# First scores of a cross-attention computed in the draining steps of the stage before it

## The reference, cut to what matters

```python
x = x + _L0_attn_ref(_layernorm(x), ...)               # linear attention: (q k^T / scale) v, no softmax
x = x + _L0_xattn_ref(ctx, ctx, _layernorm(x), ...)    # ctx has 77 rows for each sequence
...
v, k, q = (_feature_map(x, fm_w, fm_b) for x in (v, k, q))   # z = x @ fm_w.T + fm_b; concat(exp(z), exp(-z))
scores = einsum('nqhd,nkhd->nhqk', q, k) / sqrt(128.)        # 16 heads, 16 features each after the map
attn = softmax(scores, axis=-1)
out = einsum('nhql,nlhd->nqhd', attn, v).reshape(...) @ fc_w.T + fc_b
```

## Time and profile before

| | us |
|---|---|
| median of three runs | 450.48 |
| range of the runs | 449.48 to 454.25 |
| the profiled execution, its own time | 453.67 |
| its span in the profile | 451.9 |
| busy: PE, DVE, ACT, POOL | 381.6, 279.4, 255.0, 195.8 |

### The profile page before, as it was taken

One profiled execution on the slowest core, in us unless ns is written; L12 is line 12 of the kernel. 1 busy time (PEld: TensorE's weight loads), 2 busy tenths in 40 slices (PEclk: granted clock), 3 DMA queues, 4 the chain that ended last, 5 costly groups with the idle time before them and its releaser, 6 DMA issues.

```text
span 451.9 us, 10394 instructions
## 1 busy us (share of the span) xinstructions
PE 381.6 (84%) x3684; PEld 290.9 (64%) x3685; DVE 279.4 (62%) x837; ACT 255.0 (56%) x611; POOL 195.8 (43%) x280
## 2 busy tenths in 40 slices
PE   2789787897458998999989998899999978888894
PEld 1476565564226787888888887675566657667662
DVE  4667988878537688787777754727733334444436
ACT  4778889876530776777757777355632223333311
POOL 1497577753005445544630000000577717676620
PEclk9999999998755999999989999989999999999999
DMA  8962335458517667566610000000051137777529
GB/s 273 349 186 56 125 102 159 137 179 248 159 70 195 172 168 190 151 175 173 181 57 4 8 4 4 0 1 1 31 188 55 54 97 230 241 240 236 181 80 316
DMA packets 45050, 61.83 MB, mean 137 GB/s; under 512 B 7308, under 2 KB 40972, under 8 KB 43388
## 3 DMA queue, kind: packets, MB, share of 16 engines
q1 hardware_dynamic: 33400, 37.63, 27.1%
q0 software_dynamic: 4832, 20.37, 15.9%
q10 hardware_dynamic: 6768, 3.18, 2.9%
HBM read 43.34 MB, written 20.59 MB: 141 GB/s over the span
## 4 chain that ended last, share of the span: by engine, by line
PE 59%; DVE 19%; ACT 10%; issue 6%; DMA 5%; ACTq 1%; POOL 0%; DVEq 0%; SPq 0%; POOLq 0%
PE bank L743 7%; PE bank L732 6%; PE bank L1301 4%; PE bank L1356 3%; PE bank L1310 3%; PE bank L1311 3%; PE bank L705 3%; DVE res_q L348 3%; ACT xn L406 3%; DVE mx L819 3%; PE bank L767 2%; PE bank L584 2%; DMA t_row<-sorted_in 2%; PE bank L611 2%; ACT t_hT L1238 2%
## 5 line engine op out<-in xcount | busy, mean ns | idle before, releaser
L910 ACT ACTIVATE prob<-bank 77x512 f32<-77x512 f32 x128 | 74.4, 595 | 23.7 <-PE bank L732 23.5
L1282 POOL DMA_INDIRECT sorted_in<-h_rows,pos_s x32 | 31.5, 985 | 82.3 <-ACT h_rows L1215 73.7
L819 DVE TENSOR_REDUCE mx<-bank 128x5 f32<-128x385 f32 (+1 forms) x96 | 54.9, 576 | 18.6 <-PE bank L705 15.8
L1287 POOL DMA_INDIRECT routed<-t_y,t_no x47 | 45.4, 966 | 27.9 <-DVE t_y L1155 18.8
L732 PE MATMUL bank<-qst,kst 99*77 99x128 bf16 x512 | 50.8, 222 | 0.7 <-DMA qst<-mT 0.4
L1211 ACT ACTIVATE s_g<-bank 128x512 f32<-128x512 f32 x32 | 19.1, 598 | 47.3 <-PE bank L1311 33.7
L732 PEld LDWEIGHTS bank<-qst,kst 99*77 99x77 bf16 x512 | 39.0, 117 | 8.2 <-ACT prob L910 4.0
L667 POOL DMA_DIRECT2D qst<-qparts x36 | 18.2, 505 | 53.8 <-DMA kst<-kparts 34.2
L705 PE MATMUL bank<-kst,qst 96*128 96x77 bf16 x512 | 36.2, 208 | 5.8 <-DVE mx L819 3.1
L1065 DVE TENSOR_TENSOR act<-bank,s_g 128x512 f32<-128x512 f32 x24 | 16.5, 688 | 36.8 <-ACT s_g L1211 36.8
L1238 ACT COPY t_hT<-bank 128x128 f32<-128x128 f32 x47 | 12.5, 265 | 39.5 <-PE bank L1347 35.5
(11 more groups left out here) (162 smaller groups left out, 932.3 us busy)
## 6 DMA issues: line engine op xcount, KB each, us to landing
qst<-qparts POOLq DMA_DIRECT2D x36, 256.0 KB, 3.5
t_w<-in_expert_w SPq DMA_DIRECT2D x47, 192.0 KB, 2.8
qparts<-qpart SPq DMA_DIRECT2D x16, 384.0 KB, 3.9
kst<-kparts POOLq DMA_DIRECT2D x36, 154.0 KB, 4.1
kparts<-kpart SPq DMA_DIRECT2D x16, 231.0 KB, 3.7
sorted_in<-in_fill SPq DMA_DIRECT2D x1, 3102.0 KB, 12.9
t_row<-sorted_in ACTq DMA_DIRECT2D x47, 66.0 KB, 2.1
qst<-qparts SPq DMA_DIRECT2D x12, 256.0 KB, 4.4
```

Source lines behind the costliest of these rows:

```text
L819: v.tensor_reduce(mx[:, b % JA, h0:h1], bank[n % 2][:, 0:(h1 - h0) * KEYS].rearrange("p (h k) -> p h k", k=KEYS), AX.X, ALU.max, negate=Tr ...
L910: a.activation(prob[n % PROBS][:].rearrange("p c t -> p (c t)"), bank[2 + n % 2][0:KEYS], ACT.Exp, scale=SCORE_SCALE).then_inc(s["expd"], 1)
L1282: p.indirect_dma_start(out=sorted_in, out_offset=bass.IndirectOffsetOnAxis(ap=pos[:, b:b + 1].bitcast(U32), axis=0), in_=h_rows[:, b], in_ ...
L1287: p.indirect_dma_start(out=routed, out_offset=bass.IndirectOffsetOnAxis(ap=t_no[r][:].bitcast(U32), axis=0), in_=t_y[r][:], in_offset=None ...
```

## The change

Five things are edited.

- **The first scores move.** The scores of b = 0 to 3 (64 matmuls in 12 units), their maxima, the first two `parts`, the first `turn_shift` and the first `copy_shift` go from the head of stage 3 into steps 6, 7 and 8. The functions themselves stay the same, except that the first shift is transposed into bank 2.
- **The order of the sends.** SP sends the shift rows of pairs 0 and 1 before the query parts of group 7. These parts get a buffer of their own (`qhome`, on the memory of the key parts).
- **The waits for DRAM.** ACT and SP no longer wait for the last query parts at the head of stage 3. POOL loads the six query parts of group 2 without it, then waits for all, then loads the six key parts in one go, and goes on with group 3.
- **The matmuls without use** (before five, L781, ahead of the first `shifted`) are now 3 and 1 in step 7 and 4 in step 8 (`keep_streaming`, 256 columns each).
- **DVE's copy of half of V** (L379) stands ahead of `mask_products` and `query_residuals`, in the steps that have both a `front` and a `back` (steps 0 to 5).

```diff
             def step(first, front, middle, back, last):      # DVE
...
                     statistics(g, 1, "stat2", "mean2")
+                    if g >= NG - 2:
+                        for u in range(3):
+                            maxima(v, 2 * (g - (NG - 2)), u)
...
+                if front is not None and back is not None:
+                    g = front
+                    v.wait_ge(s["vp"], g + 1)
+                    v.tensor_copy(values_of(g, 1), turned_keys(g, 1)).then_inc(s["v_ready2"], 1)
                 if middle is not None:
                     mask_products(middle)
                 if last is not None:
                     query_residuals(last)
-                if front is not None and back is not None:
-                    g = front
-                    v.wait_ge(s["vp"], g + 1)
-                    v.tensor_copy(values_of(g, 1), turned_keys(g, 1)).then_inc(s["v_ready2"], 1)
...
+                    if NG - 3 <= g < NG - 1:                  # g is last
+                        k = g - (NG - 3)
+                        for u in range(3):
+                            maxima(v, 2 * k + 1, u)
+                        if k == 0:
+                            v.wait_ge(s["ones_rows"], 1)
+                        parts(v, k)
...
             def query_high(g, hf):                            # ACT
-                if g >= 2:
+                if g == NG - 1:
+                    for par in range(2):
+                        a.wait_ge(k_sent[par][hf], NG // 2 * 16)
+                        a.wait_ge(k_sent[par][1 - hf], NG // 2 * 16)
+                elif g >= 2:
                     a.wait_ge(q_sent[g % 2][hf], g // 2 * 16)
...
                     normalise(back, 1, "bias2", xn2[back % 2], "xn2")
+                if back == NG - 1:
+                    copy_shift(a, 0)
...
+                    if g == NG - 3:                           # PE, g is last
+                        pe.wait_ge(s["v_ready"], NG)
+                        for u in range(3):
+                            scores(pe, 0, u)
+                    if g == NG - 2:
+                        scores(pe, 1, 2)
+                        for u in range(3):
+                            scores(pe, 2, u)
+                        turn_shift(pe, 0)
+                        for u in range(2):
+                            scores(pe, 3, u)
+                        keep_streaming(3)
+                    if g == NG - 1:
+                        scores(pe, 3, 2)
+                        keep_streaming(4)
...
                     i.then_inc(s["mwp"], 1)                   # g is middle
+                    if g == NG - 1:
+                        scores(pe, 1, 0)
+                        scores(pe, 1, 1)
...
                     i.then_inc(s["xT2p"], 1)                  # g is back
+                    if g == NG - 1:
+                        keep_streaming(1)
...
                     for hf in range(2):                       # SP, q is last
+                        if q == NG - 1 and hf == 0:
+                            send_shift(sp, 0)
+                            send_shift(sp, 1)
                         sp.wait_ge(s["qlo"], q * 2 + (hf + 1))
...
-            all_sent(p, NG // 2)                              # POOL
             p.wait_ge(s["vp"], NG)
-            for group in range(2, NG):
+            p.wait_ge(s["xT2"], NG)
+            for i in range(len(Q_PART)):
+                load_one(p, 2, i, qst, qparts, Q_PART)
+                if i < JP:
+                    add_bias(JA + i)
+            all_sent(p)
+            for i in range(len(K_PART)):
+                load_one(p, 2, i, kst, kparts, K_PART)
+            for group in range(3, NG):
```

More of the change, by code:

```diff
@@ L536, in pe_phase1, with keep_streaming @@
         def pe_phase1(pe):
+            def keep_streaming(n):
+                for _ in range(n):
+                    pe.matmul(bank[5][:, 0:2 * P], ident[:], second_pack[:, 0:2 * P], start=True, stop=True)
             def turn_x(g):
@@ L661, in shifts, with load_one @@
             return (g // 2 + 1) * (16 * JA)
+        def load_one(eng, group, i, dst, src, part):
+            eng.dma_start(dst[group % NBUF][i:ROWS:len(part)], src[group, part[i]]).then_inc(parts_in[i % 2], 16)
         def load(eng, group, i):
@@ new lines, in decoder_layer, with scores @@
+        SHIFT_BANK = (2, 7)
+        def scores(pe, b, u):
+            r, c = home(b // JA, b % JA)
+            h0, h1 = UNITS[u]
+            n = b * len(UNITS) + u
+            if u == 0 and b % JP == 0 and b < 2 * JP:
+                pe.wait_ge(early_in[b // JP], LOADS)
+            if u == 0 and b % JP == 0 and b >= 2 * JP:
+                for k in range(2):
+                    pe.wait_ge(parts_in[k], loads(b // JA))
+            if n >= 2:
+                pe.wait_ge(s["amax"], n - 1)
+            for h in range(h0, h1):
+                i = pe.matmul(bank[n % 2][:, (h - h0) * KEYS:(h - h0 + 1) * KEYS],
+                              qst[r][0:ROWS, h, c * S:(c + 1) * S], kst[r][0:ROWS, h, c * KEYS:(c + 1) * KEYS],
+                              start=True, stop=True)
+            i.then_inc(s["ap"], 1)
```

177 lines of the change are left out of this document (77 added, 100 removed), and 6 rows, old and new, of the table s.

## The result

The changed kernel took 445.63 us, the median of four runs (442.30 to 447.90), beside 452.37 us for the kernel before on the same chip (449.48 to 455.21). The ratio is 0.9862 with an interval of 0.9819 to 0.9906. A second sitting gave 445.33 us, 0.9764 [0.9692, 0.9837]. The kernel is faster by 1.4 to 2.4%, some 7 us. Forecast were 11.85 us, a time of 438.6; the 445.63 lies above the range of 435.8 to 444.0.

The account below looks back on a forecast made before the run. A serial tail, one engine at a time and mostly at 1.2 GHz, bounds the kernel until the first `shifted`. 2.2 + 10.55 - 0.9 = 11.85 us off the profiled 453.67, shifted to the median: 438.6 us, range 435.8 to 444.0.

Parts of the forecast that it names:

- T0: Start of the first `shifted`, head of stage 3: 146.95 us before, forecast 136.4 without the gain from V's copy.
- The copy of V, 2.2 us: Steps 1 to 5: copying in DVE's idle time brings the bias 0.60 us sooner; 4 x 0.40 + 0.60 = 2.2 us.
- 0 (another engine binds within 0.1 us): Lower bound on the gain from moving DVE's copy of V; the upper bound was 3.0 us.
- The tail, 10.55 us: Steps 6 to 8: scores moved into the serial tail bring T0 from 146.95 to 136.4, 10.55 us earlier.
- Step 7: DVE's order there delays the bias of group 7 from 123.45 to 129.0: the tail loses 5.5 us.
- The first rival (442.1): Step 8: the clock does not come back, T0 = 140.7, gain 8.4 us, time 442.1; chance 0.18.
- Given back, 0.9 us: After T0: DVE's first maximum of b = 4 comes late for PE; 0.9 us charged, between 0 and 1.5.
- DVE's debt: DVE enters stage 3 later relative to T0; its first b = 4 maximum at T0 + 2.9, PE wanting T0 + 2.1.
- Loads, nothing: POOL's query and key loads in stage 3 cost nothing; sequence 4's key loads have a thin cover of 1.0 us.
- Key loads late: Stage 3: sequence 4 waits 2.5 us for key loads, group 3 again as much; time 443.6, chance 0.10.
- POOL's loads pace: Stage 3: every group waits for its loads, 12.5 us over groups 3 to 7; time 454, chance 0.04.
- their rival: Head of stage 3: shift rows' signal comes behind POOL's query loads, T0 = 139.2, time 441.0; chance 0.10.

Follow-up runs that it names:

- the rearranged kernels: Changed kernel with DVE's addition, statistics and bias of group 7 ahead of the last b = 1 maximum: 444.84 us; DVE's later parts and maxima also reordered: 440.28 us.
- the filled changed kernel: Changed kernel plus three matmuls without use in TensorE's idle 1.20 us at the end of stage 3: 445.29 us, ratio to before 0.9805.
- The kernel with the maxima first: Changed kernel with DVE's first two maxima of b = 4 ahead of group 7's middle and low parts: 441.02 us, ratio to before 0.9722.
- the freed key loads: The kernel with the maxima first, plus group 7's query parts on qkv's memory, so POOL's key loads need not wait: 444.50 us, ratio to before 0.9814.

## Why the prediction was wrong

**What bounds the kernel: right.** The tail's serial chain set T0, and T0 was worth its full amount: what lay between the fourth and the last `attend` did not grow (115.74 against 116.49).

**The copy of V, 2.2 us: wrong, 0.** The step that failed: "the bias comes 0.60 us sooner". In step 1 the bias did start 0.61 us sooner behind the mask (2.65 us instead of 3.26), but it took 0.73 us instead of 0.15 and ended as late as before. Its price came from a row in which the copy of V stood between the residuals and it while POOL read SBUF. The bound "0 (another engine binds within 0.1 us)" held, for another reason.

**The tail, 10.55 us: right in sum, 11.4.** Step 7 was dear, as forecast: the bias of group 7 stood at 128.35. Less the late start of this execution (106.45 against 105.90) that is 4.35 us later than the 123.45 of before, where the text put 5.5 on the old clock. The first `shifted` came at 136.15, not at 134.2: 2.2 of the copy's gain are missing, 0.55 is the late start, and the tail itself was 0.8 better. The clock did come back, the last L642 took 1.98 us, and the kernel without the useless matmuls shows that they brought it back. The first rival (442.1) falls. That unit (1,2), behind a slow L642, would leave DVE idle for 5.02 us was in the order and not seen as time to be had: the rearranged kernels put the addition there.

**Given back, 0.9 us: wrong, 2.2 and more.** The step that failed here: the charge for DVE's debt counted a wait alone. The wait of PE was priced right in kind and roughly in size (1.51 us, where the text said under 1). The clock fell behind it, and that cost again, 0.7 us in this profile; in the profile of the filled changed kernel it was low for 10 us, and T0 to the `attend` of b = 3 took 20.74 us. The kernel with the maxima first took the wait away and gained 4.3 us, 1.4 to 3.9 of them traced to this head.

**Loads, nothing: right, and near the edge.** PE waits for no load at b = 4 or b = 8; POOL's key loads went at 145.27, T0 + 9.1, where the text put T0 + 7.0 and a cover of 1.0 us. "Key loads late" and "POOL's loads pace" fall. The shift rows did not set T0; that their rival's mechanism exists is made likely by the row of the freed key loads, and not shown.

**End of stage 3, not in the sum.** This stretch was put at nothing, and it took 1.6 to 3.3 us more in the two profiles. Nothing in the prediction asked what happens to the clock where PE idles 1.20 us.

**The account** of the profiled spans: 11.85, less 2.2 (V), less 1.3 (2.2 given back, not 0.9), less 3.3 (end of stage 3), and plus 0.8 (tail) and 1.6 (the rest: 0.75 from the fourth `attend` on, 1.37 at the end, 0.55 lost at the start) makes 7.4, as read. By medians it is 6.7. The rest's 1.6 lies where no edit acts: it is luck of these two profiles and hides part of the miss. What stays open is how much of the clock loss at the end of stage 3 is chance.

**Slips in the text's sums.** By the earlier trace rows group 3 is wanted at T0 + 30.9, not T0 + 31.2; the middle of 3.8 and 9.6 us from 132 is 138.7, not 139.2; the "3 us of the rival above" are 2.5 or 5 there; the chances add up to 0.99. None of them moves the forecast.

## What to carry to other kernels

A short wait of TensorE can have two prices, itself and the clock behind it. At the head of stage 3, waits of 1.4 to 2.6 us were followed by some 3 to 10 us at the low clock in every profile that has one, and waits of 0.8 to 1.1 us by none. When work is moved to an earlier start, look at the first waits after that start and take them away, for they can cost more than they last. Before an instruction is moved on an engine, ask what it was shielding: the same operation next to another neighbour may last five times as long. And note each run's mean granted clock beside its time: here it goes with half of the variance between runs of one kernel (0.74 squared), and hints at which edits worked through the clock.

## What the runs showed of the hardware

- DVE's bias on 128 x 4 elements took 0.15 us, and 0.65 to 0.73 us right behind the residuals while POOL read SBUF; two residuals (128 x 512, two SBUF inputs) 1.28 us alone and up to 2.44 us beside POOL.
- The same idle stretch of TensorE (1.20 us) was followed by different clocks from run to run: no fall, or some 3.4 or 10.2 us at 1.2 GHz. The fall is read in the steps behind the idle stretch; only in the longer wait of 2.62 us did it begin within it (0.76 from 138 to 140).
- With eight matmuls of 256 columns that compute nothing ahead of it, the last feature matmul took 1.98 us; without them it took 3.78.
- Shift rows (two DMAs of 12 KB for each pair) were waited for 0.35 us behind six loads, and 1.78 us, in one profile, behind twelve.
